# Third attention: second exponentials in SBUF, two banks for scores, three in turn for the tiles of maxima

## What is computed

```python
def _mha(q_in, k_in, v_in, wq, bq, wk, bk, wv, bv):
    Q, K, V = split(q_in @ wq + bq, Sq), split(k_in @ wk + bk, Sk), split(v_in @ wv + bv, Sk)   # 16 heads of 32
    scores = jnp.einsum('bhqd,bhkd->bhqk', Q, K) / HD ** 0.5
    probs = jax.nn.softmax(scores, axis=-1)
    ctx = jnp.einsum('bhqk,bhkd->bhqd', probs, V)
    return ctx.transpose(0, 2, 1, 3).reshape(B, Sq, D)

h = _mha(x, encoder_hidden_states, encoder_hidden_states, ca_wq, ca_bq, ca_wk, ca_bk, ca_wv, ca_bv)
x = _ln(x + h, ln2_g, ln2_b)
```

## Time and profile before

| | us |
|---|---|
| median of 3 runs | 3278.21 |
| lowest, highest | 3267.07, 3283.9 |
| profiled execution | 3278.91 |
| its span, first to last instruction | 3277.1 |

### The profile page before, as it was taken

One profiled execution on the slowest core, in us unless ns is written; L12 is line 12 of the kernel. 1 busy time (PEld: TensorE's weight loads), 2 busy tenths in 40 slices (PEclk: granted clock), 3 DMA queues, 4 the chain that ended last, 5 costly groups with the idle time before them and its releaser, 6 DMA issues.

```text
span 3277.1 us, 87025 instructions
## 1 busy us (share of the span) xinstructions
PE 3004.1 (92%) x34642; PEld 2383.4 (73%) x34642; DVE 2572.7 (79%) x4750; ACT 2000.3 (61%) x4650; POOL 1260.6 (38%) x1139
## 2 busy tenths in 40 slices
PE   7998999998899869999999999999889999999996
PEld 4887888887889747777778778787766556565562
DVE  5776778888899858999999899999856666666666
ACT  2554555666778627777777777787754435444352
POOL 0454431136765743444443444443122223232222
PEclk9999999998999889999999999999999999999998
DMA  4566655446654645655655655564441221212212
GB/s 119 173 188 213 191 173 153 146 133 191 182 174 139 165 113 127 145 133 138 144 124 135 137 133 144 133 141 101 138 151 33 49 55 46 54 44 52 56 39 48
DMA packets 447330, 405.86 MB, mean 124 GB/s; under 512 B 272496, under 2 KB 354544, under 8 KB 445776
## 3 DMA queue, kind: packets, MB, share of 16 engines
q1 hardware_dynamic: 446672, 400.04, 46.0%
q10 hardware_dynamic: 256, 0.26, 0.0%
HBM read 239.98 MB, written 109.52 MB: 107 GB/s over the span
## 4 chain that ended last, share of the span: by engine, by line
PE 46%; DVE 18%; DMA 15%; ACT 8%; SPq 5%; issue 5%; POOL 3%; ACTq 0%; POOLq 0%; DVEq 0%
PE at_ps L768 19%; PE at_ps L1429 4%; PE at_ps L854 4%; DVE at_mx_cross L987 3%; DVE at_p L996 3%; PE at_ps L910 3%; PE at_ps L1443 3%; PE at_ps L1454 3%; PE at_ps L889 3%; DMA self_spill<-at_proj 2%; PE at_ps L1410 2%; DMA causal_spill<-at_proj 2%; ACT at_ps L944 2%; DMA at_stacks<-at_mrow 2%; DMA at_o_raw<-at_values 2%
## 5 line engine op out<-in xcount | busy, mean ns | idle before, releaser
L996 DVE TENSOR_TENSOR at_p<-at_ps,at_p 125x448 f16<-125x448 f32 (+2 forms) x1280 | 750.7, 596 | 146.7 <-ACT at_ps L944 137.3
L943 ACT ACTIVATE at_p<-at_ps 125x448 f16<-125x448 f32 (+2 forms) x1280 | 678.5, 530 | 302.8 <-PE at_ps L889 191.0
L944 ACT ACTIVATE at_ps<-at_ps 125x448 f32<-125x448 f32 (+2 forms) x1280 | 680.5, 532 | 0.0
L987 DVE TENSOR_REDUCE at_mx_cross<-at_ps 128x1 f32<-128x750 f32 x512 | 477.0, 932 | 29.6 <-PE at_ps L854 27.3
L1069 POOL TENSOR_TENSOR at_o_sum<-at_o_raw 128x256 f32<-128x256 f32 x192 | 121.4, 632 | 878.3 <-ACT at_o_raw L950 878.0
L910 PE MATMUL at_ps<-at_values,at_p 112*128 112x65 f16 (+3 forms) x6656 | 304.7, 186 | 22.8 <-DVE at_p L996 10.5
L1477 ACT ACTIVATE at_masks<-at_ps,at_b_cols 128x256 f32<-128x256 f32 x224 | 107.0, 478 | 337.4 <-PE at_ps L1410 337.4
L991 DVE TENSOR_REDUCE at_mx<-at_ps 112x2 f32<-112x448 f32 (+1 forms) x512 | 304.0, 610 | 9.5 <-PE at_ps L864 7.4
L1410 PE MATMUL at_ps<-at_xt,at_early 128*128 128x256 f16 x1792 | 302.3, 276 | 8.3 <-ACT at_w_first L1478 5.5
L910 PEld LDWEIGHTS at_ps<-at_values,at_p 112*128 112x128 f16 (+1 forms) x6656 | 268.4, 97 | 48.3 <-DVE at_p L996 19.3
L1429 PE MATMUL at_ps<-at_w_second,at_w_first 128*128 128x512 f16 x896 | 283.6, 379 | 0.0
(11 more groups left out here) (200 smaller groups left out, 6887.3 us busy)
## 6 DMA issues: line engine op xcount, KB each, us to landing
at_x_res<-x SPq DMA_DIRECT2D x124, 256.0 KB, 3.0
cross_spill<-at_proj SPq DMA_DIRECT2D x64, 487.0 KB, 3.2
at_x_rows<-x SPq DMA_DIRECT2D x92, 256.0 KB, 3.3
at_prep<-bit SPq DMA_DIRECT2D x32, 512.0 KB, 4.5
at_early<-ctx SPq DMA_DIRECT2D x32, 512.0 KB, 5.2
at_stacks<-cross_spill SPq DMA_DIRECT2D x64, 243.5 KB, 3.7
causal_spill<-at_proj SPq DMA_DIRECT2D x64, 224.0 KB, 2.9
at_stacks<-causal_spill SPq DMA_DIRECT2D x128, 112.0 KB, 2.2
```

The lines of the kernel that those rows point to most:

```text
L943: act.activation(mem.p_hi[0:self.KC, n % 4, 0:self.P_COLS], scores, ACT.Exp, scale=EXP_SCALE)
L944: act.activation(scores, scores, ACT.Exp, scale=EXP_SCALE).then_inc(self.exp_done, 1)
L987: dve.tensor_reduce(self.mx[:, at, t, h:h + 1], mem.ps_qk[:, :, 0:self.KT // 2], AX.XY, ALU.max).then_inc(self.max_done, 1)
L996: dve.tensor_tensor(mem.p_lo[0:self.KC, n % 4, cols], mem.ps_st[0:self.KC, self.st_bank(b, g, n), cols], mem.p_hi[0:self.KC, n % 4, cols], ...
```

## The change

In the third attention alone, four things change. First, the second exponential (L944) is written to a new ring of four places in SBUF, `p_full`, float32 (three places in the part of `stacks` that this attention leaves free, one in a tile of its own), and the subtraction L996 reads it there, not in PSUM. Second, scores have two banks (5 and 6) instead of three, and the scores of pair m wait for the second exponential of pair m-2 instead of the subtraction of pair m-3. Third, the tiles of maxima have three banks (2 to 4): the first half of a tile goes to bank 2 or 4 in turn, the second half always to bank 3, and only the second half waits for the reduction of the tile before; the reduction reads banks 2 and 3 or 3 and 4. Fourth, the first tile of the third attention waits once until the second attention's subtractions are done, since its banks overlap theirs. The first two attentions and the feed-forward keep their code.

```diff
+        self.p_full = [stacks[:, n:n + 4 * T].bitcast(F32) for n in (7792, 8688, 9584)] + [sb("p_full", [P, 2 * T])[:, :]]
+        self.cross_qk, self.cross_st = ps[:, 2:5, :], ps[:, 5:7, :]
...
+    def st(self, b, g, n):
+        if self.cross:
+            return self.mem.cross_st[0:self.KC, self.pair(b, g, n) % 2, 0:self.P_COLS]
+        return self.mem.ps_st[0:self.KC, self.pair(b, g, n) % ST_RING, 0:self.P_COLS]
+
+    def st_released(self, b, g, n):
+        pair = self.pair(b, g, n)
+        if not self.cross:
+            return self.lo_done, pair - ST_RING + 1
+        return (self.exp_done, pair - 1) if pair - self.pair0 >= 2 else (self.lo_done, self.pair0)
+
+    def exps(self, b, g, n):
+        return self.mem.p_full[self.pair(b, g, n) % 4][0:self.KC, :] if self.cross else self.st(b, g, n)
+
+    def qk_banks(self, b, g, n):
+        return 2 * (self.tile(b, g, n) % 2), 1
+
+    def qk(self, b, g, n):
+        low, high = sorted(self.qk_banks(b, g, n))
+        return self.mem.cross_qk[:, low:high + 1, 0:self.KT // 2]
...
-            if self.cross or n == 0 and g == 0 and b == self.b0:
-                wait(pe, self.max_done, self.tile(b, g, n))
+            if n == 0 and g == 0 and b == self.b0:
+                wait(pe, self.max_done, self.tile0)
+                if self.cross:
+                    pe.wait_ge(self.lo_done, self.pair0)
...
-                for half in range(2):
-                    last = pe.matmul(mem.ps_qk[:, half, 0:KT // 2], qs[0:96, h, TILES[t]:TILES[t] + P],
+                for half, bank in enumerate(self.qk_banks(b, g, n)):
+                    if half == 1:
+                        wait(pe, self.max_done, self.tile(b, g, n))
+                    last = pe.matmul(mem.cross_qk[:, bank, 0:KT // 2], qs[0:96, h, TILES[t]:TILES[t] + P],
                                      ks[0:96, h, half * KT // 2:(half + 1) * KT // 2], start=True, stop=True)
...
-            wait(pe, self.lo_done, m - ST_RING + 1)
+            wait(pe, *self.st_released(b, g, n))
...
-            act.activation(scores, scores, ACT.Exp, scale=EXP_SCALE).then_inc(self.exp_done, 1)
+            act.activation(self.exps(b, g, n), scores, ACT.Exp, scale=EXP_SCALE).then_inc(self.exp_done, 1)
...
-                dve.tensor_reduce(self.mx[:, at, t, h:h + 1], mem.ps_qk[:, :, 0:self.KT // 2], AX.XY, ALU.max
+                dve.tensor_reduce(self.mx[:, at, t, h:h + 1], self.qk(b, g, n), AX.XY, ALU.max
...
-            dve.tensor_tensor(mem.p_lo[0:self.KC, n % 4, cols], mem.ps_st[0:self.KC, self.st_bank(b, g, n), cols],
+            dve.tensor_tensor(mem.p_lo[0:self.KC, n % 4, cols], self.exps(b, g, n)[:, cols],
                               mem.p_hi[0:self.KC, n % 4, cols], ALU.subtract).then_inc(self.lo_done, 1)
```

More of the change, by code:

```diff
@@ L568, in vs @@
         return self.values[self.place(b, g)]
-    def st_bank(self, b, g, n):
-        return self.pair(b, g, n) % ST_RING
+    def st(self, b, g, n):
[14 more added lines that the diff above has]
+        return self.mem.cross_qk[:, low:high + 1, 0:self.KT // 2]
     def by_scalar(self, kind):
@@ L875, in tensor @@
                     pe.wait_ge(self.slots_set, 2 * g + 2)
-            m = self.pair(b, g, n)
-            wait(pe, self.lo_done, m - ST_RING + 1)
-            bank = self.st_bank(b, g, n)
+            wait(pe, *self.st_released(b, g, n))
+            st = self.st(b, g, n)
             h, c0 = n // (NCH // 2), 2 * (n % (NCH // 2))
             if self.causal:
-                early, late = mem.ps_st[0:KC, bank, 0:T], mem.ps_st[0:KC, bank, T:T + P]
+                early, late = st[:, 0:T], st[:, T:T + P]
                 pe.matmul(early, ks[:, h, 0:KC], qs[:, h, 0:T], start=True, stop=False)
@@ L888, in tensor @@
                     at = (c - c0) * T
-                    last = pe.matmul(mem.ps_st[0:KC, bank, at:at + T], ks[:, h, c * KC:(c + 1) * KC], qs[:, h, 0:T],
+                    last = pe.matmul(st[:, at:at + T], ks[:, h, c * KC:(c + 1) * KC], qs[:, h, 0:T],
                                      start=True, stop=True)
@@ L941, in scalar @@
             wait(act, self.pv_done, m - 3)
-            scores = mem.ps_st[0:self.KC, self.st_bank(b, g, n), 0:self.P_COLS]
+            scores = self.st(b, g, n)
             act.activation(mem.p_hi[0:self.KC, n % 4, 0:self.P_COLS], scores, ACT.Exp, scale=EXP_SCALE)
-            act.activation(scores, scores, ACT.Exp, scale=EXP_SCALE).then_inc(self.exp_done, 1)
+            act.activation(self.exps(b, g, n), scores, ACT.Exp, scale=EXP_SCALE).then_inc(self.exp_done, 1)
         elif kind == "evacuate":
```

## The result

The changed kernel takes 3453.42 us (median of 4 runs, 3442.65 to 3467.91), the one before 3281.06 us in the same comparison: a ratio of 1.0536, 95% interval [1.0505, 1.0567], so +172 us. The forecast was +150 (3429 us). The profiled execution of the changed kernel took 3467.9 us with a span of 3466.1, at the upper end of its runs. In the changed file the lines have moved: L996 is now L1023, L987 is L1014, L854 is L882, L889 is L916, L910 is L937, L944 is L971.

The account below looks back on a forecast made before the run. The prediction took TensorE and VectorE, both almost full and waiting for each other, to bound the third attention. Half tile -10, score banks +10, SBUF reads 0 and lock +150 gave +150, so 3429 us, range 3335 to 3550.

Parts of the forecast that it names:

- The lock: Third attention: the subtraction, with two SBUF inputs, stands still until GpSimd's running operation is over; +150 us.
- 187 us standing still: Third attention: VectorE's total time held at the subtractions, summed along the trace before; 15 of it under one-input GpSimd operations.
- 0.8 of it reaches the end: Third attention: of the 187 us that VectorE stands still, 0.8 lengthens the kernel, taken as +150 us.
- The bound of +78: Third attention: least cost if every idle VectorE microsecond vanishes; as the rival of a mostly absorbed lock, 3340 us, chance 0.13.
- The range's lower end: Whole kernel: 3335 us, from the lower bound less the larger half-tile gain and some scatter.
- Half tile +, score banks -: Third attention, TensorE: half a tile of maxima ahead gains 10 us, two score banks instead of three cost 10.
- Two SBUF inputs by themselves: 0: Third attention's subtraction: reading both inputs from SBUF costs 0 without GpSimd beside it, bounds +-8 us.
- The exponential to SBUF: 0: Third attention, ScalarE: writing the second exponential to SBUF instead of PSUM costs nothing and adds no wait.
- TensorE's clock: Third attention, rival: held subtractions stop TensorE often enough that its clock falls to 1.2 GHz; 3483 to 3563 us, chance 0.14.
- No lock: Third attention, rival: GpSimd lets the subtraction pass and the half tile pays; 3252 to 3262 us, chance 0.05.
- the next rival: Third attention: without a lock, the score banks take the half tile's gain back; 3282 to 3295 us, chance 0.06.
- The signs named in advance: Trace after: subtraction median near 0.62 us, mean near 0.85; VectorE over 95% busy, TensorE near 85%; longer GpSimd operations; rest unchanged.

Follow-up runs that it names:

- e8: The changed kernel with the third attention's long GpSimd operations each cut into four of a quarter of the columns: 3349 us, ratio 1.0214.
- e2: The kernel before with only the SBUF ring for the second exponential, banks for maxima and scores as before: 3468 us, ratio 1.0569.
- e10: The kernel before with only the SBUF ring, banks as before, and most of the third attention's GpSimd work left out: 3288 us, ratio 1.0037.
- e3: The changed kernel with most of the third attention's GpSimd work left out (2 of 512 columns from the second batch element on): 3307 us, ratio 1.0084.
- e5: The changed kernel with four more GpSimd additions of the shift per batch element of the third attention, same result: 3522 us, ratio 1.0742.
- e4: The kernel before with most of the third attention's GpSimd work left out (2 of 512 columns from the second batch element on): 3273 us, ratio 0.9987.
- e11: The kernel before with GpSimd's last bias in the feed-forward waiting until VectorE has rounded the next rows: 3266 us, ratio 0.9973.

## Why the prediction was right, step by step

- **The lock.** Right, and with the sign. The case rested on twelve instructions of another layer and shape; the runs that take away, add, cut up and replace GpSimd's reads move the held time and the time together.
- **187 us standing still.** Measured 209. The sum went along the trace before, where subtractions and GpSimd lay as they then did; once both engines take turns, the hits move, and 192 subtractions were held instead of 177 operations met. The error is all in the one-input operations: the 15 us put down to them were really 42 (L1074, L1076, L1086, L1088 held 61 subtractions), while the rest, 172 in the sum, came out at 167. Before, 49 subtractions start under these four lines, after it 78.
- **0.8 of it reaches the end.** The stage grew by 177 us for 209 held, 0.85, and VectorE's idle time gave 17 of the 152 us it had. Other runs with the lock lie to both sides: 0.76 in e8 (77 us of stage for 101 held), 0.92 in e2 (189 for 206); in all of them banks and clock have a part. The bound of +78, with all idle time used, was far off; the reason given (idle time that consists of waiting for each other is no spare time) holds. This is the term of the sum that was undersized, together with the one before: 150 for 177. The range's lower end, 3335 us, is 5 us above its own sum (3279 + 78 - 27 = 3330); nothing hung on it.
- **Half tile +, score banks -.** Taken as -10 and +10. With the lock nearly gone they are about -18 and +21 at TensorE's matmuls, but +19 us in all (e10 to e3): the sum of the two was off by those 19 us, since 7 us of waiting for the stacked operands and 8 us of busy time had no term. Under the lock the sign may turn, as 12 us between the stages of e2 and the change suggest; the times don't show it.
- **Two SBUF inputs by themselves: 0.** Right: the median is 625 and 621 ns for 619 in the mean before. The 50 us saved, estimated from the Trainium skill's "VectorE: DVE Perf Modes", section "The TRN2 errata", are not seen.
- **The exponential to SBUF: 0.** Right: in the mean 547 ns to the first of the ring's two tiles and 561 to the second, 546 to PSUM before.
- **TensorE's clock.** A rival of its own in the prediction; here it came along in small. Between 1240 and 2560 us there are 21 stretches at 1.2 GHz, 96 us in all, none between 1240 and 2360 before. Each comes after two held subtractions of 1.4 to 2.8 us. One of them, with the 10 us ahead of it:

```profile
2228.00:2238.00 10.00, 6.29 (x97) 5.39 (x98) 9.74 (x11) 4.88 (x12) 4.96 (x2) 1.00 0.87 179
2238.00:2241.40 3.40, 3.40 (x40) 3.02 (x39) 2.74 (x5) 2.41 (x6) 0.00 (x0) 0.52 1.10 230
```

TensorE was busy 6.3 of the 10 us, then throughout, at 0.52. VectorE idles 19 of the 96 us, where at the stage's rate it would 7; by that reckoning some 12 of the 177 us hang on the clock. It is an estimate: no run takes the clock away and leaves the lock, and TensorE's busy time in the stage grew by 56 us with the same matmuls. Over the whole stage the time at 1.2 GHz is 50 us before, 133 in the change, 156 in e2, 245 in e5 and 57 in e8. So the hold is paid without the slow clock too: e8, with nearly the clock of before, loses 77 us of stage to 101 us held.

- **No lock.** The rival on the other side gave 3252 to 3262 us for a half tile that pays freely. It falls twice: the lock is there, and with nearly all of it gone (e3) the change is still 34 us slower than the kernel before (e4). By an estimate, 23 us held at 0.85 are 20 of these 34; the 14 that are left are what the next rival, in which the score banks take the gain back, gave (3 to 16 us).
- **The signs named in advance.** Met: the subtraction's median (0.62 us) and mean (0.89 for "near 0.85"), its ends after GpSimd's, L987, L943 and L944 unchanged, TensorE at 85% of the stage, longer GpSimd operations, the other parts as before. Not met: VectorE over 95% busy. It is busy 91% of the stage (88% before), so most of its idle time stayed, as the 0.85 says.

## What to carry to other kernels

Moving an operand of a VectorE instruction from PSUM to SBUF frees a bank, but if the other operand is in SBUF already, the instruction can no longer run while GpSimd reads SBUF; count the GpSimd operations that would lie over it, and their length, before the banks. In a trace, look for one short VectorE instruction with a few durations of several times its median (four times for the subtraction, fourteen for L1525), and for what GpSimd did at those moments. Where such a pair can't be avoided, cut GpSimd's operations into short ones, or put them where the hold matters less, as e11 did with one of them; where VectorE has instructions with one SBUF input there is none.

## What the runs showed that was not expected

Idle time of 12% on VectorE (152 of 1241 us) took up only 17 of 209 us: these two engines, in a tight exchange, had next to no reserve. A GpSimd operation that is added to a crowded place costs less than the ones already there (94 us held by the new ones, 62 us more in all), since it moves its neighbours. And write-only GpSimd operations beside the change made it some 20 us faster, only in part by way of the held time; how the rest came about wasn't tried.
